# A graph network kernel on one core: byte offsets as record columns, 32 registers a load, and more gather tiles fetched row by row

## The reference, cut to what matters

```python
# L0: attention over edges, softmax by dst, gated with a skip
a   = einsum('ehd,ehd->eh', q[src], k[dst]) / sqrt(D);  sa = softmax of a over the edges of each dst
agg = segment_sum(v[src] * sa, dst)
# L1: relations, both directions, mean for each type
xw  = einsum('ni,rio->rno', x, weight)
agg = segment_sum(xw[et_all, src_all], et_all * n + dst_all)
out = sum(agg / deg over the 8 types) + x @ self_weight
# L2: messages summed for each src
agg = segment_sum(x[ei[1]] + edge_attr @ W_edge + b_edge, ei[0]);  then a two-layer MLP with batch norm
# L3: messages summed for each dst
segment_sum(x[src] @ W + b + edge_attr_6 @ We + be, dst)
```

## Time and profile before

| | us |
|---|---|
| median of 3 runs | 21862.58 (21862.25 to 21864.21) |
| span of the profiled execution, first to last instruction | 15054.0 |
| the profiled execution's own time | not given beside its span |
| GpSimd busy | 11087.4 (74%) |
| VectorE busy | 9778.7 (65%) |
| TensorE busy | 8740.4 (58%) |
| ScalarE busy | 2787.6 (19%) |

### The profile page before, as it was taken

One profiled execution on the slowest core, in us unless ns is written; L12 is line 12 of the kernel. 1 busy time (PEld: TensorE's weight loads), 2 busy tenths in 40 slices (PEclk: granted clock), 3 DMA queues, 4 the chain that ended last, 5 costly groups with the idle time before them and its releaser, 6 DMA issues. The chain is left out here.

```text
span 15054.0 us, 271220 instructions
## 1 busy us (share of the span) xinstructions
PE 8740.4 (58%) x56159; PEld 6734.5 (45%) x56575; DVE 9778.7 (65%) x34050; ACT 2787.6 (19%) x7303; POOL 11087.4 (74%) x11347
## 2 busy tenths in 40 slices
PE   6766667777777777555555555555444444544444
PEld 2212226666666666244444444444333333433334
DVE  8877777777878778866666677777533333433334
ACT  0011114444444444421111111111100000200000
POOL 4777767777777777777777777777677777477776
PEclk8866668999999999865555555555555555655555
DMA  2011122222222222422222222222222222422222
GB/s 85 7 42 50 53 59 74 69 69 69 69 69 69 69 69 67 152 83 59 59 58 59 58 63 63 62 63 63 69 63 63 63 62 60 121 59 59 58 59 68
DMA packets 734382, 992.39 MB, mean 66 GB/s; under 512 B 271737, under 2 KB 534898, under 8 KB 732626
## 3 DMA queue, kind: packets, MB, share of 16 engines
q0 software_dynamic: 387968, 670.55, 17.1%
q1 hardware_dynamic: 324786, 301.13, 6.5%
q10 hardware_dynamic: 20000, 3.33, 0.1%
HBM read 795.25 MB, written 178.86 MB: 65 GB/s over the span
## 5 line engine op out<-in xcount | busy, mean ns | idle before, releaser
L1834 DVE TENSOR_TENSOR acc<-banks,acc 128x128 f32 x3328 | 969.8, 291 | 2616.2 <-PE banks L1792 2247.3
L668 POOL DMA_INDIRECT rec_dst<-stage_dst_sort,row_dst_sort x1563 | 1575.4, 1008 | 641.1 <-issue 474.3
L800 POOL DMA_INDIRECT far_att<-table_qv,recs_att x1664 | 1636.5, 983 | 523.9 <-issue 506.8
L800 POOL DMA_INDIRECT far_sum_dst<-table_h,recs_dst x1613 | 1561.2, 968 | 584.1 <-issue 491.7
L800 POOL DMA_INDIRECT far_sum_src<-table_h,recs_src x1613 | 1572.9, 975 | 558.8 <-issue 491.6
L800 POOL DMA_INDIRECT far_rel_src<-table_xw,recs_rel_src x1638 | 1574.7, 961 | 508.7 <-issue 494.2
L800 POOL DMA_INDIRECT far_rel_dst<-table_xw,recs_rel_dst x1638 | 1561.1, 953 | 510.4 <-issue 494.5
L1622 DVE TENSOR_TENSOR acc<-banks,acc 128x128 f32 x3328 | 969.7, 291 | 1119.2 <-PE banks L1548 1002.5
L936 POOL DMA_INDIRECT rec_src<-moved_att,row_src x1248 | 1245.0, 998 | 397.3 <-issue 379.9
L1792 PE MATMUL banks<-far_sum_src,hot_sum_src 128*128 128x128 f32 x3226 | 825.1, 436 | 1214.9 <-DVE hot_sum_src L1825 831.3
L1792 PE MATMUL banks<-far_sum_dst,hot_sum_dst 128*128 128x128 f32 x3226 | 825.9, 436 | 1147.5 <-DVE hot_sum_dst L1825 899.8
(11 more groups left out here) (343 smaller groups left out, 21302.0 us busy)
## 6 DMA issues: line engine op xcount, KB each, us to landing
lone_sync_rel_dst<-table_xw SPq DMA_DIRECT2D x3328, 0.5 KB
lone_sync_rel_src<-table_xw SPq DMA_DIRECT2D x3328, 0.5 KB
lone_sync_sum_src<-table_h SPq DMA_DIRECT2D x3328, 0.5 KB
lone_sync_sum_dst<-table_h SPq DMA_DIRECT2D x3328, 0.5 KB
lone_scalar_sum_src<-table_h ACTq DMA_DIRECT2D x3200, 0.5 KB
lone_scalar_sum_dst<-table_h ACTq DMA_DIRECT2D x3200, 0.5 KB
table_xw<-xw_rel_tables SPq DMA_DIRECT2D x98, 512.0 KB
far_att<-table_qv,recs_att POOLq DMA_INDIRECT x1664
```

The costliest lines, as they stand in the source:

```text
L668: e.indirect_dma_start(out=flat_dst, out_offset=bass.IndirectOffsetOnAxis(ap=row["dst"][:, c + i:c + i + 1], axis=0), in_=stage["dst"][:, ...
L800: e.indirect_dma_start(out=self.far[:, g % RING, t, :], out_offset=None, in_=table, in_offset=bass.IndirectOffsetOnAxis(ap=index, axis=0)) ...
L1834: e.tensor_tensor(acc[:, bass.ds(at[t], 1), :], sums[g0 % 4][:, t:t + 1, :], acc[:, bass.ds(at[t], 1), :], ALU.add).then_inc(k.s_sum, 1)
```

## The change

The records get two columns more in place of one: `OFF` is the far node's number times 512, `OFF8` is `IDX8` times 512, both written by ScalarE in the sort. These are the byte offsets at which the rows begin in the two tables. A record is 12 or 22 numbers instead of 11 or 21. The single-row DMA takes the table as a flat array of bytes and the register as it is for the start. 32 offsets are read into registers at once instead of 8, and they stay there when a block's share ends between. A lone tile is the last of groups 9, 19, 29 and so on: 41 tiles in each of the four passes for SyncE, and for ScalarE in the sum passes 41, the last but one of groups 13, 23 and so on. SyncE's share for a block is 51 or 52 rows; ScalarE's is now 12 or 13 rows a group, and its two copies stand between them at fixed groups. In the relation passes SyncE's two buffers lie in memory that the sort no longer needs. GpSimd leaves out the same tiles.

```diff
-IDX, IDX8, LOC, TYP, ONE, ATT = range(6)
+IDX, IDX8, LOC, TYP, OFF, OFF8, ATT = range(7)
+ROW = F * 4
+LOAD = 32
...
             e.copy(to[:, b, 0:n, TYP], typ[:, c:c + n])
+            e.activation(to[:, b, 0:n, OFF].bitcast(I32), node[FAR[s]][:, c:c + n], ACT.Copy, scale=float(ROW))
+            e.activation(to[:, b, 0:n, OFF8].bitcast(I32), idx8[s][:, c:c + n], ACT.Copy, scale=float(ROW))
             e.wait_ge(s_att[s][b], 16 * (j // 2 + 1))
-            e.copy(to[:, b, 0:n, ATT:], att[s][:, b, 0:n, :]).then_inc(s_staged[s], 1)
+            e.copy(to[:, b, 0:n, ATT:ATT + ATTRS[s]], att[s][:, b, 0:n, :]).then_inc(s_staged[s], 1)
...
+class Lone:
+
+
+    def __init__(self, buffer, ids, column, tile, first, step):
+
+        self.buffer, self.ids, self.column, self.tile, self.step = buffer, ids, column, tile, step
+        self.groups = list(range(first, GROUPS, step))
+        self.at = None
...
-        if g % LONE != LONE - 1:
-            return None
-        name = {GT - 1: "sync", GT - 2: "scalar"}.get(t)
-        return name if name in self.lone and (name == "sync" or g >= LONE) else None
+        for name, one in self.lone.items():
+            if t == one.tile and g in one.groups:
+                return name
+        return None
...
-    def number_rows(self, e, name, s, column):
-
-        tile = (s * LONE + LONE - 1) * GT + self.mine(name)
-        done = sum(self.lone_base[name]) // P + 16 * (self.turns(name, s) + (self.turns(name, s - 1) if s else 0) - 1)
+                s = self.lone[name].groups.index(g)
+                e.wait_ge(self.k.s_lone[name][s % 2], self.lone_base[name][s % 2] + 16 * P * (s // 2 + 1))
+
+    def number_rows(self, e, name, s):
+
+        one = self.lone[name]
+        tile = one.groups[s] * GT + one.tile
         with self.k.nc.allow_non_contiguous_dma(reason="one number of each record"):
-            e.dma_start(self.ids[name][0:1, s % 2, :], self.rec[:, tile, column:column + 1].bitcast(I32).rearrange("p c -> c p")).then_inc(self.k.s_ids[name], 16)
-        return done + 16
-
-    def fetch_rows(self, e, name, s, table, first, n):
-
-        for p in range(first, first + n, 8):
-            row = e.bass.values_load_multi_w_load_instructions(
-                self.ids[name][0:1, s % 2, p:p + 8], engines=[e.engine], min_val=0, max_val=table.shape[0] - 1,
-                skip_runtime_bounds_check_because="the sort writes numbers of rows of the table alone")[1]
-            for i in range(8):
-                e.dma_start(self.lone[name][p + i:p + i + 1, s % 2, :], table[bass.ds(row[i], 1), :]).then_inc(self.k.s_lone[name][s % 2], 16)
+            e.dma_start(one.ids[0:1, s % 2, :], self.rec[:, tile, one.column:one.column + 1].bitcast(I32).rearrange("p c -> c p")).then_inc(self.k.s_ids[name], 16)
+
+    def single_rows(self, e, name, g, n, table, freed):
+
+        one = self.lone[name]
+        r, end = (min(P * h // one.step, P * len(one.groups)) for h in (g, g + n))
+        width = table.shape[1] * 4
+        flat = table.rearrange("n f -> (n f)").bitcast(U8)
+        while r < end:
+            s, first = divmod(r, P)
+            m = min(P - first, end - r)
+            if first == 0:
+                if s == 0:
+                    self.number_rows(e, name, 0)
+                if s >= 2:
+                    e.wait_ge(*freed(one.groups[s - 2]))
+                e.wait_ge(self.k.s_ids[name], self.ids_base[name] + 16 * (s + 1))
+                if s + 1 < len(one.groups):
+                    self.number_rows(e, name, s + 1)
+            for p in range(first, first + m):
+                if p % LOAD == 0:
+                    one.at = e.bass.values_load_multi_w_load_instructions(
+                        one.ids[0:1, s % 2, p:p + LOAD], engines=[e.engine], min_val=0, max_val=(table.shape[0] - 1) * width,
+                        skip_runtime_bounds_check_because="the sort writes where rows of the table begin alone")[1]
+                row = flat[bass.ds(one.at[p % LOAD], width)].rearrange("(a n) -> a n", a=1)
+                e.dma_start(one.buffer[p:p + 1, s % 2, :].bitcast(U8), row).then_inc(self.k.s_lone[name][s % 2], 16)
+            r += m
...
+        spent = [k.row_src[:, 2 * i * F:2 * (i + 1) * F].rearrange("p (b f) -> p b f", b=2) for i in range(2)]
+        lone = {"sync": Lone(spent[0].bitcast(F32), spent[1][0:1, :, :], OFF8, GT - 1, 9, 10)}
...
                 st.load(e, c)
                 if c:
-                    single_rows(c - 1)
-            single_rows(BLOCKS - 1)
+                    st.single_rows(e, "sync", (c - 1) * RG, RG, k.table_xw, freed)
+            st.single_rows(e, "sync", GROUPS - RG, RG, k.table_xw, freed)
...
+        old = k.inverse[0:1, :, :].rearrange("p w r -> p (w r)")[:, -2 * P:].bitcast(I32).rearrange("p (b n) -> p b n", b=2)
+        lone = {"sync": Lone(sb("lone_sync", [P, 2, F]), old, OFF, GT - 1, 9, 10),
+                "scalar": Lone(sb("lone_scalar", [P, 2, F]), sb("ids_scalar", [1, 2, P], I32), OFF, GT - 2, 13, 10)}
...
+            for g in range(GROUPS):
+                j = beside(g, 5)
+                if j is not None:
+                    b, m = j % 2, WIN4[j][1] * P
+                    e.wait_ge(k.s_etr, f0 + j + 1)
+                    if j >= 2:
+                        e.wait_ge(k.s_ec, f0 + j - 1)
+                    e.copy(et[:, b, 0:m], k.psum[4 + b][0:n_more, 0:m]).then_inc(k.s_et, 1)
+                j = beside(g, 10)
+                if j is not None and not gine:
+                    b, m = j % 2, WIN4[j][1] * P
                     e.wait_ge(k.s_ec, f0 + j + 1)
                     e.copy(k.conv[j], k.psum[6 + b][:, 0:m].rearrange("p (n f) -> p n f", f=F)).then_inc(k.s_spent, 1)
-
-                s = j + 1
-                if s >= LONES:
-                    continue
-                if s >= 3:
-                    e.wait_ge(k.s_product, p0 + (s - 1) * LONE)
-                e.wait_ge(k.s_ids["scalar"], numbered[s])
-                if s + 1 < LONES:
-                    numbered[s + 1] = st.number_rows(e, "scalar", s + 1, IDX)
-                st.fetch_rows(e, "scalar", s, k.table_h, 0, P)
+                st.single_rows(e, "scalar", g, 1, k.table_h, freed)
```

More of the change, by code:

```diff
@@ L71 @@
 EPS = 1e-5
[L73 removed]
+F32, BF16, I32, I16, U8 = mybir.dt.float32, mybir.dt.bfloat16, mybir.dt.int32, mybir.dt.int16, mybir.dt.uint8
 ACT = mybir.ActivationFunctionType
@@ L305, in sort_edges @@
         blank = {s: sb(f"blank_{s}", [P, BT, COLS[s]]) for s in SIDES}
-        att = {s: sb(f"att_{s}", [P, 2, CH, COLS[s] - ATT]) for s in SIDES}
+        att = {s: sb(f"att_{s}", [P, 2, CH, ATTRS[s]]) for s in SIDES}
         stage = {s: sb(f"stage_{s}", [P, 2, CH, COLS[s]]) for s in SIDES}
@@ L807, in far_rows @@
         name = self.fetcher(g, t)
-        return self.lone[name][:, g // LONE % 2, :] if name else self.far[:, g % RING, t, :]
+        if name is None:
+            return self.far[:, g % RING, t, :]
+        one = self.lone[name]
+        return one.buffer[:, one.groups.index(g) % 2, :]
     def fetched(self, e, g):
@@ L849, in close @@
         self.k.rec_base += 16 * (BLOCKS // NREC)
-        if self.far is not None:
-            self.k.ring_base = [self.gathered(GROUPS - RING + r)[1] for r in range(RING)]
-        for name in self.lone:
+        self.k.ring_base = [self.gathered(GROUPS - RING + r)[1] for r in range(RING)]
+        for name, one in self.lone.items():
+            self.k.ids_base[name] += 16 * len(one.groups)
             for b in range(2):
-                self.k.lone_base[name][b] += 16 * P * self.turns(name, LONES - 2 + (LONES - 2 + b) % 2)
+                self.k.lone_base[name][b] += 16 * P * len(range(b, len(one.groups), 2))
 assert BLOCKS % NREC == 0 and GROUPS % RING == 0
@@ L874, in attention_pass @@
         top = sb("top", [P, W + 1, H])
-        st = Stream(k, "dst", sb("recs", [P, NREC, BT, CD]), sb("far", [P, RING, GT, 2 * F]))
+        st = Stream(k, "dst", sb("recs", [P, NREC, BT, CD]), sb("far", [P, RING, GT, 2 * F]), {})
         win = k.win["dst"]
@@ L1475, in relation_pass @@
         p0, q0, b0 = k.passes * GROUPS, k.relations * GROUPS, k.relations * BLOCKS
+        freed = lambda g: (k.s_product, p0 + g + 1)
         def sync(e):
-            numbered = {}
-            def single_rows(c):
-                share = P * RG // LONE
-                r, end = c * share, (c + 1) * share
-                while r < end:
-                    s, first = divmod(r, P)
-                    n = min(P - first, end - r)
-                    if first == 0:
-                        if s == 0:
-                            numbered[0] = st.number_rows(e, "sync", 0, IDX8)
-                        if s >= 2:
-                            e.wait_ge(k.s_product, p0 + (s - 1) * LONE)
-                        e.wait_ge(k.s_ids["sync"], numbered[s])
-                        if s + 1 < LONES:
-                            numbered[s + 1] = st.number_rows(e, "sync", s + 1, IDX8)
```

(12 more changed lines are left out.)

48 lines of the change are left out of this document (7 added, 41 removed).

## The result

| | before | after |
|---|---|---|
| median, us | 21863.4 (21862.25 to 21889.69, 4 runs) | 23004.68 (22999.89 to 23038.0, 4 runs) |
| ratio | | 1.0521, 95% interval 1.0506 to 1.0536 |
| span of the profiled execution, us | 15054.0 | 23002.0 (its own time: 23003.75) |

Slower by 1141 us; the forecast was +1207, 23070.

The account below looks back on a forecast made before the run. GpSimd's list of gathers was taken to bound the four passes before, SyncE's rows after. Passes of +304 twice and +300 twice, plus 2 in the sort, made +1210 on 21863: 23073, say 23070 us; range 21690 to 23400.

Parts of the forecast that it names:

- SyncE becomes the end of each pass: Relation and sum passes: SyncE works 2347 us, longer than GpSimd's gathers, and sets the end: +304 us twice, +300 twice.
- The signs: Profile after: no FUSED_REGOPS, 164 loads of 2.8 to 3.1 us, SyncE's waits near zero, passes of about 2370 us.
- The price of a row: SyncE's single-row DMAs: 0.412 us per row before, 0.336 after, because the FUSED_REGOPS, taken as the product, goes.
- The load of 32: SyncE's load of 32 registers: 2.89 us taken, bounds 0.781 and 3.4, since time goes with the number of registers.
- I take it to lie around the span and to stay: Whole kernel: the 6809 us between profiled span 15054 and median 21863 lie outside the span and don't change.
- 250 us of room: Relation pass before: SyncE works 1810 us of 2060; the change spends what is left.
- 24 behind the last lone tile: Relation pass end: seven groups follow the last lone tile (group 409), at 3.4 us each some 24 us.
- Rival 2: The 6809 us lie inside the passes, on GpSimd's gathers (period 1.85 us), hiding SyncE's 2347: 21690 us; chance 0.10.
- rival 1: Four passes: a row is much cheaper than counted and GpSimd stays the bound: 117 us less, 21746; chance 0.12.
- rival 3: Single rows are dearer: FUSED_REGOPS stays, 24670 us, or a load of 32 takes 6.4 us, 25370; chance 0.04.
- rival 4: Four passes: SyncE comes out at GpSimd's old length (load near 1 us), time within 0.2%; chance 0.04.
- ScalarE in the sum passes: ScalarE's single rows take 2180 us a sum pass, over GpSimd's 2025 but under SyncE's 2347: no cost by itself.

Follow-up runs that it names:

- Experiment 4: The changed kernel, with GpSimd gathering only the first eight groups of each of the four passes: 18757.12 us, beside 22202.36 for the kernel before.
- experiment 7: The changed kernel with the multiplication of row number by row size put back, 41 tiles and loads of 32 kept: 25602.23 us, ratio 1.1515 to the kernel before.
- experiment 3: The changed kernel with loads of 8 registers instead of 32, 41 tiles kept: 23422.67 us, ratio 1.0743 to the kernel before.
- experiment 2: The changed kernel with 26 lone tiles instead of 41 for each fetching engine and pass: 20383.87 us, ratio 0.9349 to the kernel before.
- experiment 6: The changed kernel with no lone tiles, all 1664 tiles of each pass gathered by GpSimd: 19623.84 us, ratio 0.8838 to the kernel before.
- experiment 1: The kernel before, unchanged, timed again and profiled a second time: 21798.6 us, ratio 1.0, span 21796.0 us.

## Why the prediction was right in its number, and where it was wrong

**SyncE becomes the end of each pass: right for after.** The signs came that its waits are near zero, that there is no FUSED_REGOPS, that a pass has 164 loads, and that most of GpSimd's idle time is no longer "issue". Only the first bears on the bound, and the kernel before has it too once it is profiled in a long execution. The others failed: GpSimd waits for the record loads themselves, not for TensorE's products (four blocks of them do not hide the queue), TensorE waits for SyncE's rows in the sum passes alone, the load is under 2.8 us, and the passes are 3153 to 3405 us and not 2370.

**The price of a row: right.** Experiment 4 leaves SyncE alone and gives 2224 against a list of 2220 (with the load as measured). That the FUSED_REGOPS was the product and the MOVE stays is shown by experiment 7.

**The load of 32: the term was too large.** 2.89 was taken, 2.12 measured, 66 ns per register; inside the bounds, and below the value that the slope from four to eight gave. It is 164 x 0.77 = 126 us a pass too much. With the right load the sum would have given near 22570. The Trainium skill's rule of 200 ns per register, which the prediction set beside it ("Runtime: NRT & Kernel Launch", section "Instruction fetch mechanics"), is three times what the change shows. The Trainium skill writes there of loads that the runtime puts in, which read HBM ("Terms" on the same page); these read SBUF, so it may be another case. And what the larger load saves was read too high: three crossings of 0.13 go, but three steps between rows come in their place (experiment 3). The sum doesn't use that sentence. It also took 2066 us for both sum passes, where the stretch of the second, 12953 to 15012, is 2059.

**"I take it to lie around the span and to stay": wrong, and the real error.** The 6809 us lie inside: 1.1 ms in the sort, 1.6 in the attention pass, 0.8 to 1.0 in each of the four passes. So GpSimd's list was not what set the passes of the kernel that is timed, and SyncE had no 250 us of room to spend. What replaces the step, in the first relation pass:

- Forecast: own work of SyncE +537 (2347 - 1810), less the 257 of room in the pass of 2067, plus 24 behind the last lone tile = +304.
- Measured: own work +410 (2220 - 1810), less 106 by which the rest fell (1079 to 973) = +304.

The forecast has 127 us too much of own work, the load, and takes 233 off for room and end, where 106 went, by smaller stretches. That the two errors are equal is luck; the right step with the wrong load, or the wrong step with the right load, would each have missed the number by some 500 us over the four passes. What was earned is that SyncE's rows set the pass after, their price, and so the sign and the rough size. Taken apart by experiment 2, the change is +660 for 15 tiles (own work 787) and -356 for the row form and the larger load (own work 377).

**Rival 2 had the premise, and a part of the mechanism.** It put the missing time into the passes, by a longer period of GpSimd's gathers, which would hide SyncE. The gathers take 944 ns (947 before), but without single rows their mean period is 1.48 us and not 1.25, because GpSimd waits for products (experiment 6). It isn't the 1.85 that the rival needed, SyncE is stretched more, and so its forecast of 21690 failed. "Spans and runs of one program are the same instructions" was true and proved nothing: the same instructions took 15054 and 21796 us.

**Rivals 1, 3 and 4** needed a row or a load much cheaper or dearer than listed. The load came nearest, at 2.12 us, where rivals 1 and 4 needed 1.0 or less.

**ScalarE in the sum passes.** Not the end, as said: SyncE's rows are what TensorE waits for. The sort is 33 us longer than in the second profile against an estimate of 2, but experiments 2 and 3, with the same two added instructions, have 3210 and 3181 against 3204: they can't be told apart.

**Shown and open.** Shown: SyncE's stretches and TensorE's late semaphores come with GpSimd's gathers, between two stages of one execution (experiment 4), and for the stretches from one stop of GpSimd to the next. Not shown: what in a gather causes them; whether it is the work of GpSimd or its 128 rows in flight was not separated, nor whether the writing of the trace's own records has a part, since every timed execution has a recorded span. Why the first profile had neither is open too. The nine later profiles, of all kernels, are alike in the sort (3181 to 3287 us) and the attention pass (5338 to 5385), and none is near its 2075 and 3781.

**The version to keep** is none of the two: the kernel without single rows, 11.6% faster than before, and 0.8838 / 1.0521 = 0.84 of the change's time. It still has the wider records; without them it wasn't run. Fetching 128 rows one at a time costs SyncE 4 x 12.93 = 52 us and saves one gather, 1.48 us of that pass.

## What to carry to other kernels

Hold the span of a profile against the time of the runs before reading anything else; when they differ by a third, profile again before a bound is named, for the engine that looks like the bound may not be it. Price work on an engine that only issues DMAs (its busy time isn't on the page) by sequences in its timeline, then test the price by taking the other engines' work away. When a wait has no releaser, look which semaphore the waiting instruction names, and how long after its instruction's end that semaphore rose. And before tuning a side path, measure the kernel without it.

## What the runs showed of the hardware

- A load of 32 registers takes 2.12 us on SyncE and 2.26 on ScalarE, 66 and 71 ns per register, against 98 and 104 for 8 in the earlier trace rows. The medians are the same with the gathers left out (2.12 and 2.26).
- While GpSimd gathers, SyncE's queue stands still at times for 0.7 or 1.4 us, within instructions that otherwise take 29 to 228 ns or between them; ScalarE's does too (8.3% of its MOVEs over 500 ns in the second profile, none in the first). It adds 0.9 to 1.2 ms to a pass of some 1630 gathers that SyncE sets. With the gathers left out 4 us remain, and from 3 us after the last gather on it is rare: 4 times in 1092 us (experiment 4).
- In the same executions TensorE's semaphores rise late while GpSimd gathers: 3.6 to 3.8 us (median) after the matmul in the attention pass of all nine later profiles, 2.4 to 4.9 in the first relation pass of those with gathers there. In the first profile, and in experiment 4's passes without gathers, it is 14 ns.
- The mean granted TensorE clock of the attention pass differs too. The first profile of before, and of after (length, busy by engine, clock, DMA share and GB/s at the end):

```profile
2200.00:6000.00 3800.00, 2762.69 (x25975) 2392.95 (x26387) 3022.13 (x11198) 1541.47 (x4145) 2879.71 (x2910) 0.91 0.26 70
```

```profile
4000.00:8000.00 4000.00, 2668.66 (x19882) 2260.04 (x19883) 2225.12 (x8391) 1156.26 (x3110) 2103.35 (x2176) 0.77 0.18 49
```

The granted clock was 0.91 there and 0.77 here. TensorE's late semaphores account for most of the longer pass (experiment 1); what the clock adds was not separated.
